# A two-layer graph network on one core: the 256-column products of the gather stages as two of 128 columns

## The chip, the cores and the metric

The kernel runs on one core of a Trainium2 chip, as one program. The metric is the device time in microseconds (us) of that core, taken from several executions. A profile of one execution shows what each engine did. The engines are called PE (TensorE, matmuls), PEld (its weight loads), DVE (VectorE), ACT (ScalarE), POOL (GpSimd) and SP (SyncE, which here only issues DMAs).

## The reference

3125 nodes with 128 features and 100000 edges (src, dst), sorted by dst. Two SAGE layers come first, then a layer norm, then two PNA layers, then a layer norm. What matters here is the sums over each node's incoming edges:

```python
# SAGE layer (twice)
summed = segment_sum(x[src], dst)
mean = summed / max(deg, 1)
x @ W_self + mean @ W_neigh + b
# PNA layer (twice)
h = (x @ W_pre[:F])[dst] + (x @ W_pre[F:])[src] + b_pre
mean = segment_sum(h, dst) / degc
mean_sq = segment_sum(h * h, dst) / degc
std = sqrt(relu(mean_sq - mean * mean) + EPS_VAR)
mx, mn = segment_max(h, dst), segment_min(h, dst)
agg = concat([mean, mx, mn, std])
out = concat([x, agg, agg * amp, agg * att]) @ W_post + b_post
```

## The kernel before

The nodes stand in NT = 25 blocks of NB = 125. A sum over edges is a product with a matrix of counts: for a block b of destinations and a block a of sources, the counts `A[:, slot, a, :]` (125 x 128, bf16) are the operand that is loaded into TensorE, and the rows of the source block stream past. A row in f32 is split into three bf16 parts c, so a block b takes 25 x 3 = 75 products that add up in one bank of PSUM (`acc[:, bank, 0:width]`). The helper is `add_block`; its line in the profile is L1190. It is called in three places:

- in the counting stage, with `width` = F = 128, inside a hardware loop;
- in `second_sums` (the second SAGE layer), with `width` = F, all 75 products of a block in a row;
- in `main_scan`, once for each PNA layer, with `width` = 2F = 256: columns 0 to 127 are the rows, 128 to 255 their squares. These two calls are the gather stages, the longest part of the program.

A gather stage is cut by hand into NSLOT = 91 slots. In a slot s TensorE does, in this order: `select` for slot s+1 (six products of 500 columns that pick rows for the maximum and minimum, L1305); at some slots the operands of a finished block (L1276 to L1279, f32, and transposes, L1266); some pieces of the sums ahead (a piece is one a, three products); `lift_absent` (two products of 500 columns, L1317); and more pieces behind it. The tables AHEAD and BEHIND fix the number of pieces: 0, 2 or 4 ahead, 5 to 7 behind. VectorE does `take_top` (L2228) after `select`, some rows of a running maximum (`scan_row`, L2275), `take_low` (L2246) after `lift_absent`, and more rows. `select` of slot s+2 waits for `take_low` of slot s, and `lift_absent` of slot s waits for `take_top` of slot s.

Beside this, POOL gathers the rows for `scan_row` from memory, four rows to a batch (`gather_rest`, L1129, an indirect DMA for each row), into a ring of six batches; ACT negates them (L947); SP writes the scanned rows out (L654), and the ring's place is free when that write is done. ACT copies the finished sums of a block (L786) and then loads the counts of the block after next (A<-counts). SP loads `picks` for `select`.

Of the kernel before, what the change touches and what calls it, by code (L numbers as in the profile page):

```python
# [14 lines left out]
F = 128  # L15
N = 3125
E = 100000
NB = 125
NT = N // NB
# [192 lines left out]
def gnn_kernel(nc, x, src, dst, w_self1, w_neigh1, b1, w_self2, w_neigh2, b2,  # L212
# [3 lines left out]
    with ctx:  # L216
        def sb(name, shape, dt=F32):
            return ctx.enter_context(nc.sbuf_tensor(name, shape, dt))
# [28 lines left out]
        XS = big[:].bitcast(BF16).rearrange("p (a c f) -> p a c f", c=3, f=2 * F)  # L247
        EXT = big[:, 0:NT * 2 * F].rearrange("p (a f) -> p a f", f=2 * F)
        A = sb("A", [P, 2, NT, P], BF16)
# [158 lines left out]
        acc = ps[:, 0:5]  # L408
# [765 lines left out]
        def _(pe):  # L1174
# [8 lines left out]
            def add_block(k, b, bank, slot, width, a0, a1):  # L1183

                if a0 == 0:

                    pe.wait_ge(sums_out, b + (NT * k + 1))
                for a in range(a0, a1):
                    for c in range(3):
                        m = nc.tensor.matmul(acc[:, bank, 0:width], A[0:NB, slot, a, :], XS[0:NB, a, c, 0:width],  # L1190
                                             start=a == 0 and c == 0, stop=a == NT - 1 and c == 2)
                if a1 == NT:
                    m.then_inc(summed, 1)

# [12 lines left out]
            def make_block(b, slot, first=False):  # L1207

                for j in range(PIECES):
                    pe.wait_ge(onehots, b * (2 * PIECES) + (2 * j + 3))  # L1210
                    pe.wait_ge(counted, b * PIECES + (j + 1))
                    h = (slot + j) % 2
                    for t in range(PT):
                        at = t // WT * CODES
                        m = nc.tensor.matmul(acc[:, h, at:at + CODES], hot_s[:, h, :, t],  # L1215
                                             hot_c[:, h, t],
                                             start=t % WT == 0, stop=t % WT == WT - 1)
                    m.then_inc(tallied, 1)
                    if first and 0 < j < COLS:
                        turn_windows(j)  # L1220
                    if not first and j > 1:
                        pe.wait_ge(counts_made, b * NG + (j - 1 - NG))
                        add_block(0, b - 1, 3 - slot, 1 - slot, F, (j - 2) * GT, (j - 1) * GT)
# [13 lines left out]
            with pe.Fori(0, NT // 2) as i:  # L1237
                make_block(i * 2 + 1, 1)
                make_block(i * 2 + 2, 0)
            pe.wait_ge(counts_made, NT * NG)  # L1240
            add_block(0, NT - 1, 2, 0, F, 0, NT)
            pe.wait_ge(pe_go, 4)
            nc.tensor.matmul(acc[:, 3, 0:P], tiny[:, 4:5].to_broadcast([P, P]), ident[:],
                             start=True, stop=True)
            pe.wait_ge(upper_made, 2)
            nc.tensor.matmul(acc[:, 3, P:2 * P], run_count.to_broadcast([P, P]), upper,
                             start=True, stop=True).then_inc(small_mm, 1)
# [74 lines left out]
            def main_scan(l):  # L1322
# [9 lines left out]
                def piece(b, a):  # L1332
                    if b == 0 and a % GT == 0:
                        pe.wait_ge(squares_ready, NG * l + a // GT + 1)
                    if a == 0:
                        pe.wait_ge(a_in[b % 2], 16 * (b // 2 + 1 + (k - 1) * ((NT + 1 - b % 2) // 2)))
                    add_block(k, b, b % 2, b % 2, 2 * F, a, a + 1)
# [1128 lines left out]
```

## Time and profile before

| | |
|---|---|
| median of 3 runs | 2146.79 us |
| lowest, highest run | 2123.44, 2160.79 us |
| profiled execution | 2106.36 us |
| its span, first to last instruction | 2104.6 us |
| PE busy | 1443.8 us (69%), 11250 matmuls |
| PEld busy | 1041.9 us (50%), 11250 loads |
| DVE busy | 1423.3 us (68%) |
| POOL busy | 804.5 us (38%) |
| mean granted clock of TensorE | 0.863 |

Busy shares are means over stages that differ much. A view by stage tells where an engine waits; the chain of waits tells what ended last. The two gather stages run from about 636 to 1262 us and from 1365 to 1985 us of the span. A matmul's recorded time holds the way of its last column through the array, so the cost of one in a row of many is the distance of the starts and not the mean.

### The profile page before, as it was taken

How to read it: one execution, taken by the hardware profiler on the slowest of the kernel's cores; microseconds unless marked ns; L12 is line 12 of the kernel's file. 1: busy time of each engine (PE TensorE's matmuls, PEld its weight loads, DVE VectorE, ACT ScalarE, POOL GpSimd, SP SyncE). 2: the span in 40 equal slices, each digit the busy share in tenths (PEclk: the TensorE clock that was granted, in tenths of full speed). 3: DMA queues.
4: the chain of work that ended last, by engine and by line, in shares of the span. 5: the costliest groups of instructions: out<-in, count | busy, mean ns of one | idle time of the engine just before them, and what ended most of it. 6: DMA issues, size and time to landing. Idle time of an engine off the chain costs nothing.

```text
span 2104.6 us, 30157 instructions
## 1 busy us (share of the span) xinstructions
PE 1443.8 (69%) x11250; PEld 1041.9 (50%) x11250; DVE 1423.3 (68%) x2879; ACT 502.3 (24%) x1074; POOL 804.5 (38%) x831
## 2 busy tenths in 40 slices
PE   0267777666974777877777865636777887787564
PEld 0156777655972444545554542424444554455432
DVE  7899999783425866666666754766655776676457
ACT  3357777500112111111111110310111111111101
POOL 4400000014006455556655624065545555565230
PEclk9879888886996988989988987978888998898876
DMA  5323333322443555555656532344555565565320
GB/s 119 94 110 140 140 140 140 125 87 93 161 139 98 178 171 192 178 186 184 200 167 197 184 113 63 92 141 161 176 181 176 187 201 182 170 219 170 139 63 25
DMA packets 126252, 309.57 MB, mean 147 GB/s; under 512 B 21744, under 2 KB 73408, under 8 KB 125742
## 3 DMA queue, kind: packets, MB, share of 16 engines
q1 hardware_dynamic: 75216, 145.00, 19.7%
q10 hardware_dynamic: 23470, 105.20, 14.2%
q0 software_dynamic: 27440, 57.77, 10.0%
q8 instruction: 69, 1.13, 0.2%
q14 instruction: 57, 0.47, 0.1%
HBM read 167.18 MB, written 140.75 MB: 146 GB/s over the span
## 4 chain that ended last, share of the span: by engine, by line
DVE 34%; PE 32%; issue 14%; another core or an unknown queue 12%; DMA 3%; ACT 2%; POOL 2%; ACTq 1%; DVEq 0%; POOLq 0%
PE ps L1190 16%; PE ps L1305 6%; DVE accs L2246 5%; DVE scanned L2275 4%; DVE accs L2228 4%; DVE scanned L1769 3%; DVE scanned L1766 3%; DVE scanned L1775 3%; PE ps L1317 2%; PE ps L1215 2%; PE ps L1405 1%; DVE S L1742 1%; DMA A<-counts 1%; ACT Y L756 1%
## 5 line engine op out<-in xcount | busy, mean ns | idle before, releaser
L1129 POOL DMA_INDIRECT scanned<-table,rest_idx x688 | 675.2, 981 | 712.1 <-DMA rest_history<-scanned 248.1
L1190 PE MATMUL ps<-big,A 125*128 125x128 bf16 (+1 forms) x7500 | 756.0, 257 | 60.9 <-issue 49.4
L1190 PEld LDWEIGHTS ps<-big,A 125*128 125x128 bf16 x7500 | 622.9, 103 | 190.9 <-issue 83.4
L1305 PE MATMUL ps<-S,big 126*128 126x500 bf16 (+1 forms) x1050 | 276.2, 406 | 251.7 <-DVE accs L2246 171.0
L2246 DVE TENSOR_TENSOR accs<-accs,ps 128x1000 f32<-128x1000 f32 (+1 forms) x154 | 166.7, 1083 | 342.7 <-remote 257.1
L2275 DVE SCALAR_TENSOR_TENSOR scanned<-scanned,rest_neg 128x256 f32<-128x256 f32 x688 | 331.7, 482 | 40.6 <-issue 7.6
L1305 PEld LDWEIGHTS ps<-S,big 126*128 126x128 bf16 x1050 | 101.1, 106 | 371.3 <-DVE accs L2246 187.5
L1215 PE MATMUL ps<-scanned 128*128 128x150 bf16 x1050 | 115.6, 252 | 76.3 <-DVE scanned L1775 75.4
L2228 DVE TENSOR_TENSOR accs<-accs,ps 128x1000 f32<-128x1000 f32 (+1 forms) x154 | 165.9, 1077 | 1.8 <-DVE sums_t L1883 1.3
L1148 POOL IOTA Y<- 128x784 int32 x1 | 0.8, 786 | 359.9 <-DVEq L2033 359.9
L1215 PEld LDWEIGHTS ps<-scanned 128*128 128x128 bf16 x1050 | 87.2, 132 | 92.7 <-issue 71.2
L811 ACT ACTIVATE A<-ps,tiny 128x450 bf16<-128x450 f32 x175 | 109.7, 635 | 87.6 <-PE ps L1215 47.8
L1317 PE MATMUL ps<-S,lift 128*128 128x500 bf16 (+1 forms) x350 | 102.5, 372 | 39.1 <-DVE accs L2228 19.6
L786 ACT COPY sums_t<-ps 128x128 f32<-128x128 f32 x50 | 13.3, 266 | 485.0 <-remote 271.6
L1405 PE MATMUL ps<-weights,scanned 128*128 128x384 f32 x200 | 90.8, 585 | 50.3 <-DVE scanned L2328 31.3
L947 ACT ACTIVATE scanned<-scanned 128x512 f32<-128x512 f32 x172 | 104.7, 620 | 57.6 <-DMA scanned<-table,rest_idx 49.1
L1769 DVE TENSOR_TENSOR scanned<-scanned,H 128x900 bf16<-128x900 bf16 x175 | 108.0, 617 | 0.0
L1766 DVE TENSOR_TENSOR scanned<-scanned,H 128x750 bf16<-128x750 f16 x175 | 94.5, 540 | 9.5 <-PE ps L1215 9.3
L796 ACT ACTIVATE A<-A,tiny 128x640 bf16<-128x640 bf16 x125 | 99.5, 818 | 0.4 <-DVE S L1742 0.4
L920 ACT ACTIVATE operands_t<-operands_t 128x128 f32<-128x128 f32 x50 | 15.5, 310 | 352.1 <-DVE operands_t L1876 247.3
L1775 DVE TENSOR_TENSOR scanned<-scanned,H 128x768 bf16<-128x768 bf16 x175 | 95.9, 548 | 0.0
L1405 PEld LDWEIGHTS ps<-weights,scanned 128*128 128x128 f32 x200 | 39.8, 221 | 76.9 <-DVE scanned L2328 38.8
(395 smaller groups left out, 1410.0 us busy)
## 6 DMA issues: line engine op xcount, KB each, us to landing
rest_history<-scanned SPq DMA_DIRECT2D x172, 512.0 KB
A<-counts ACTq DMA_DIRECT2D x75, 800.0 KB
S<-picks SPq DMA_DIRECT2D x60, 640.0 KB
picks<-S ACTq DMA_DIRECT2D x25, 800.0 KB
counts<-A ACTq DMA_DIRECT2D x25, 800.0 KB
scanned<-table,rest_idx POOLq DMA_INDIRECT x688
table<-Y SPq DMA_DIRECT2D x10, 320.0 KB, 2.6
S<-picks SPq DMA_DIRECT2D x10, 160.0 KB
```

What stands on the lines that cost most here:

```text
L1129: nc.gpsimd.indirect_dma_start(out=lanes[:, r, s, 0:F], out_offset=None, in_=tables[1 + l], in_offset=bass.IndirectOffsetOnAxis(ap=rest_id ...
L1190: m = nc.tensor.matmul(acc[:, bank, 0:width], A[0:NB, slot, a, :], XS[0:NB, a, c, 0:width], start=a == 0 and c == 0, stop=a == NT - 1 and ...
L1215: m = nc.tensor.matmul(acc[:, h, at:at + CODES], hot_s[:, h, :, t], hot_c[:, h, t], start=t % WT == 0, stop=t % WT == WT - 1)
L1305: m = nc.tensor.matmul(ps[:, bank + h, 0:len(blocks) * NB], XS[0:NB + 1, a, c, 0:F], pick[0:NB + 1, part % RING, 0:len(blocks), a % PART, ...
L1317: m = nc.tensor.matmul(ps[:, bank + h, 0:len(blocks) * NB], lift[:], pick[:, part % RING, 0:len(blocks), a % PART, 0:NB], start=False, sto ...
L1405: m = nc.tensor.matmul(acc[:, b % GT, 0:3 * F], lhs_ext[:, SLOT[b % GT], h * P:(h + 1) * P], weights[:, w + 4 + 3 * h:w + 7 + 3 * h, :] .r ...
L1766: v.tensor_tensor(plain_s[:, h, 0:NB], iota_s[:, 0:NB], by_step(lows, n).unsqueeze(1).to_broadcast([P, NB, PT]), ALU.is_equal)\
L1769: v.tensor_tensor(hot_c[:, h].rearrange("p t (c u) -> p t c u", u=2), iota_c.rearrange("p (c u) -> p c u", u=2).unsqueeze(1) .to_broadcast ...
L1775: v.tensor_tensor(hot_s[:, h], plain_s[:, h], by_step(heavy, n).unsqueeze(1).to_broadcast([P, P, PT]), ALU.mult)\
L2228: v.tensor_tensor(top[:, :, 0:cols], top[:, :, 0:cols], ps[:, bank:bank + 2, 0:cols], ALU.max)\
L2246: v.tensor_tensor(low[:, :, 0:cols], low[:, :, 0:cols], ps[:, bank:bank + 2, 0:cols], ALU.min)\
L2275: v.scalar_tensor_tensor(this, last, rest_neg[:, i:i + 1], this, ALU.add, ALU.max)\
```

## The change

Where `width` is 256, each product of `add_block` other than the first and the last of a block is issued as two of 128 columns, one over the rows and one over the squares, each with its own load of the same counts. The first product of a block (a = 0, c = 0) and the last (a = 24, c = 2) stay whole. Where `width` is 128, nothing changes.

```diff
                 for a in range(a0, a1):
                     for c in range(3):
-                        m = nc.tensor.matmul(acc[:, bank, 0:width], A[0:NB, slot, a, :], XS[0:NB, a, c, 0:width],
-                                             start=a == 0 and c == 0, stop=a == NT - 1 and c == 2)
+                        first, final = a == 0 and c == 0, a == NT - 1 and c == 2
+                        step = width if first or final else F
+                        for f in range(0, width, step):
+                            m = nc.tensor.matmul(acc[:, bank, f:f + step], A[0:NB, slot, a, :],
+                                                 XS[0:NB, a, c, f:f + step], start=first, stop=final)
                 if a1 == NT:
                     m.then_inc(summed, 1)
```

The order of TensorE's instructions in the middle of the first gather stage, three slots before the change. Rows of `big,A` are the products of the sums; a row with x15 stands for fifteen.

```order
L1305 MATMUL ps<-S,big 128x500 x6
L1190 MATMUL ps<-big,A 128x256 x6
L1266 MATMUL ps<-ident,operands_t 128x128 x2
L1317 MATMUL ps<-S,lift 128x500 x2
L1190 MATMUL ps<-big,A 128x256 x21
L1305 MATMUL ps<-S,big 128x500 x6
L1276 MATMUL ps<-weights,C 128x384
L1278 MATMUL ps<-weights,operands_t 128x384
L1279 MATMUL ps<-weights,operands_t 128x384
L1317 MATMUL ps<-S,lift 128x500 x2
L1190 MATMUL ps<-big,A 128x256 x15
```

Nothing has changed places afterwards; the same place, where a block ends and the next begins in the last rows (its line is L1193 now):

```order
L1308 MATMUL ps<-S,big 128x500 x6
L1193 MATMUL ps<-big,A 128x128 x12
L1269 MATMUL ps<-ident,operands_t 128x128 x2
L1320 MATMUL ps<-S,lift 128x500 x2
L1193 MATMUL ps<-big,A 128x128 x42
L1308 MATMUL ps<-S,big 128x500 x6
L1279 MATMUL ps<-weights,C 128x384
L1281 MATMUL ps<-weights,operands_t 128x384
L1282 MATMUL ps<-weights,operands_t 128x384
L1320 MATMUL ps<-S,lift 128x500 x2
L1193 MATMUL ps<-big,A 128x128 x28
L1193 MATMUL ps<-big,A 128x256
```

The 6, 21 and 15 products became 12, 42 and 28 and one whole, each on its old side of `lift_absent`; no wait and no other engine's instruction moved.

## Rows read from the trace of the kernel before

**Rows 1.** Gather stages by engine: busy us, instructions, clock, DMA share, GB/s

```profile
636.00:1262.00 626.00, 459.56 (x2824) 300.33 (x2824) 404.35 (x701) 98.05 (x250) 338.98 (x346) 0.88 0.52 172
1365.00:1985.00 620.00, 460.10 (x2818) 297.40 (x2815) 405.15 (x698) 96.74 (x248) 335.81 (x342) 0.87 0.53 175
```

**Rows 2.** Chain that ended last, by line, in the first gather stage

```profile
by line: another core or an unknown queue 17.8%; issue 14.9%; PE ps L1190 13.5%; PE ps L1305 9.8%; DVE accs L2246 9.1%; DVE scanned L2275 7.2%; DVE accs L2228 6.2%; PE ps L1317 3.7%; PE ps L1276 1.8%; PE ps L1278 1.7%; PE ps L1279 1.7%; DVE
```

**Rows 3.** PE groups by form: busy us, mean ns, idle before

```profile
L1190 PE MATMUL ps<-big,A 125*128 125x256 bf16 x3750 | 487.7, 282 | 22.9 <-issue 21.2 <-DVEq L2314 1.4
L1190 PE MATMUL ps<-big,A 125*128 125x128 bf16 x3750 | 268.3, 233 | 38.0 <-issue 28.2 <-ACT A L796 4.7 <-DMA A<-counts 4.0
```

**Rows 4.** Pieces of the chain at the full clock: start us, us

```profile
541.95 4.19 PE ps L1190 x75
...
811.84 1.64 PE ps L1190 x15
```

**Rows 5.** Timeline of PE, start us and us, a run of 128-column products at half clock

```profile
505.48 4.30 PE L1190 MATMUL ps<-big,A 125*128 125x128 bf16 x39 [0.44 <-issue]
509.61 0.60 PE L1482 MATMUL ps<-ident,sums_t 128*128 128x128 f32 x4
```

**Rows 6.** Pieces of the chain just behind a long wait

```profile
746.58 2.68 PE ps L1305 x6
749.26 2.56 PE ps L1190 x12
...
808.20 1.28 PE ps L1305 x6
```

**Rows 7.** Short stretches by engine, columns as in Rows 1

```profile
506.00:509.00 3.00, 3.00 (x31) 3.00 (x30) 0.00 (x0) 0.00 (x0) 0.00 (x0) 0.50 0.09 36
546.00:554.00 8.00, 8.00 (x141) 7.92 (x139) 5.80 (x18) 1.53 (x4) 0.00 (x0) 1.00 0.53 172
```

**Rows 8.** One line's loads: min/median/max ns

```profile
L1190 PEld LDWEIGHTS ps<-big,A x7500: 95/98/152, 120.6 to 1970.9; 125*128 125x128 bf16 x198
```

**Rows 9.** Waits in the first gather stage: us, times, longest

```profile
DVE accs L2246 <- remote: 121.3, 19, 13.3
```

**Rows 10.** The same view, PE alone: first gather stage, then the second

```profile
PE ps L1190 <- issue: 5.7, 11, 0.9
...
PE ps L1190 <- issue: 15.4, 29, 1.1
```

**Rows 11.** Timeline of POOL around one such wait

```profile
841.53 0.94 POOL L1129 DMA_INDIRECT scanned<-table,rest_idx  x1 [7.26 <-DMA rest_history<-scanned]
...
855.47 0.94 POOL L1129 DMA_INDIRECT scanned<-table,rest_idx  x1 [0.30 <-issue]
```

**Rows 12.** The same place on PE and DVE

```profile
850.07 1.80 PE L1190 MATMUL ps<-big,A 125*128 125x256 bf16 x15
...
855.09 1.20 DVE L2246 TENSOR_TENSOR accs<-accs,ps 128x1000 f32<-128x1000 f32 x1 [5.73 <-remote]
```

**Rows 13.** Stretches with POOL issuing without a pause, columns as in Rows 1

```profile
841.50:852.00 10.50, 9.22 (x61) 6.29 (x59) 7.46 (x14) 1.73 (x4) 8.03 (x9) 1.00 0.51 160
465.20:469.40 4.20, 3.88 (x66) 3.49 (x63) 4.03 (x6) 0.37 (x1) 3.29 (x4) 1.00 0.55 189
469.40:505.00 35.60, 18.21 (x132) 11.60 (x132) 21.40 (x27) 1.43 (x3) 26.61 (x25) 0.59 0.19 55
657.00:682.00 25.00, 10.34 (x39) 6.08 (x37) 11.62 (x16) 2.88 (x6) 16.49 (x16) 0.70 0.23 66
```

**Rows 14.** Chain in the second of these stretches, and at 672 us

```profile
482.43 0.58 PE ps L1190 x4
483.01 0.87 issue
...
672.03 8.86 another core or an unknown queue
```

**Rows 15.** DMA queues: packets, MB, share

```profile
q8 instruction: 69, 1.13, 0.2%
```

## Prediction

> **What bounds the kernel now.** I read the profile by stage first. The change touches only the two gather stages, 1246 us of the 2104.6 us span [rows 1]. There TensorE is busy 74% of the time and VectorE 65%; the DMA engines are at 0.52 and POOL at 54%. No engine is full, so busy shares alone don't say what a longer product costs. The chain of waits does: the products of the sums (L1190) are 13.5% of it in the first stage, the other matmuls of TensorE about 19%, the steps of VectorE on L2246, L2275 and L2228 about 22%, and 33% is "another core or an unknown queue" and "issue", in which no engine's recorded work ended last [rows 2]. The reader is to see two kinds of time here. One is steady slots of some 4.7 us, in which TensorE's instructions follow each other without a gap and VectorE fits in beside them. The other is long waits: VectorE's `take_low` waited 19 times, 121.3 us in all, for something that the trace doesn't name, in the first stage alone [rows 9].
>
> **Count.** Each stage has 25 blocks of 75 products, 3750 in both [rows 3]. Two of each block stay whole, so 3750 - 100 = 3650 products are cut and 3650 matmuls with 3650 loads are added. The columns that stream stay the same: 3650 x 256.
>
> **Cost of one cut, array time.** The trace has both forms, each with a load for every product. At the full clock fifteen 256-column products take 1.64 us, 109.3 ns each, and 75 products of 128 columns take 4.19 us, 55.9 ns each [rows 4], where the granted clock is 1.00, that is 2.4 GHz [rows 7]. Two halves are 111.7 ns, so a cut costs 2.4 ns. At half clock (0.50, 1.2 GHz [rows 7]) the 39 narrow products started 4.13 us before the next instruction, 105.9 ns each [rows 5], and twelve wide ones take 2.56 us, 213.3 ns each [rows 6]: two halves are 211.8 ns, no loss. With the mean clock at 0.88 and 0.87 [rows 1], about a quarter of the time is at half clock; I count the full price for all: 3650 x 2.4 ns = 8.8 us.
>
> **Cost of the second load.** The operand is the same one again, and no row shows a load that is left out, so it is really issued. A load is recorded with 98 ns in the median [rows 8], yet the 75 narrow products each had one and came every 55.9 ns [rows 4]. So two loads overlap, and the load's price is already in the 55.9 ns. This was measured in the second SAGE layer and not in a gather stage. The bound from above is that the loads stop overlapping when POOL gathers: 2 x 98 - 109.3 = 87 ns for each cut; from below a cut can't gain array time, since the columns are the same. I take the 2.4 ns, because the DMA load was alike (0.53 there, 0.52 and 0.53 in the gather stages [rows 1, 7]).
>
> The Trainium skill speaks against that: TensorE: Matmul & The Clock Gate, section Back-to-back issue gap, gives a sustained spacing of about 81 ns for a load with a 128-column product. By that figure a cut would cost 2 x 81 - 109 = 53 ns, an estimate of +193 us in all. The 55.9 ns of the trace decide against it here.
>
> **What lies on the path.** In steady slots TensorE's instructions have no gap between them, so all of its added time moves the next `select`. During the long waits of TensorE nothing is added, since the products are done by then. So I put 7 of the 8.8 us on the path (bounds 0 and 8.8).
>
> **Dispatch.** Inside runs of products TensorE waited for "issue" 11 times for 5.7 us and 29 times for 15.4 us, 21.1 us in both stages [rows 10]. If these pauses come by the instruction, twice as many instructions meet up to twice as many of them: 0 to +21 us. Half of such time is hidden beside VectorE, and I don't know whether the pauses come by instruction or by time, so I take +5. The instructions themselves are fetched by DMA; the larger of the two queues for them carried 1.13 MB at 0.2% of the engines' time [rows 15], and even doubled that is nothing beside 0.52. I cost it at nothing.
>
> **Other engines.** No wait is added. `summed` is still raised by the last product of a block, which stays whole; ACT's copy and the load of the next counts behind it move with TensorE. SP and POOL have the same instructions in the same order.
>
> **Sum.** +7 + 5 = +12 us. The profiled execution took 2106.4 us and would take 2118; the median of the runs is 2146.8, 40 above it, so the forecast there is 2159 us, 0.6% more. The runs differ by 37 us among themselves, so what I forecast can hardly be told from no change; about 2% is what a measurement of this kernel can tell.
>
> **Rivals.**
>
> *Long waits that come by the number of instructions (slower).* This is the one that I weigh most. Whenever POOL issues gathers without a pause, TensorE comes to a stand. From 841.53 to 855.47 us POOL issues one each 1.25 us [rows 11]; TensorE ran 61 products and 59 loads until 852 [rows 13], then `take_low` waited 5.73 us although `lift_absent` had been issued long before [rows 12]. In the second SAGE layer POOL began at about 465.2 us: TensorE ran 66 products and 63 loads in 4.2 us, then came in bursts of about four products with 0.87 us between them [rows 13, 14]. Some 120 to 130 instructions in both cases, but 10.5 us in one and 4.2 in the other: that looks like a budget of instructions. A slot has about 31 matmuls (2824 / 91) now and 51 after. The budget of about 120 (60 matmuls with their loads) would be used up after 1.2 slots and not 2.0. With 19 waits in 91 slots a cycle has 4.8 slots; 0.8 less makes 4.0, and the waits come 20% more often. I take 160 us of such waits in each stage (17.8% of 626 us is 111, and about half of "issue" [rows 2]): +64 us, with the array's 9 us 2220. It passes +43 us, the 2% bound, when the waits come 13% more often and nothing else is lost. Against it speaks the start of the first stage: from 657 to 682 us there are only 39 products and 37 loads in 25 us [rows 13], and still the chain has a wait of 8.86 us [rows 14]. There the stand can't come from many instructions; it goes by POOL's time. And in the bursts TensorE runs about a sixth of the time (4 x 55.9 ns of 1.45 us), as an engine would that is let in between POOL's instructions. Chance 0.19.
>
> *Loads exposed while POOL gathers (slower).* By the bound above 3650 x 87 ns = +318 us, 2465. It would have to show in the wide products too, and they keep 109.3 ns. Chance 0.02, and the Trainium skill's 81 ns would be a milder form of it (an estimate of 2340).
>
> *Clock (faster).* After each long wait TensorE runs at half clock: six products of `select` take 2.68 us and not 1.28, twelve of the sums 2.56 [rows 6] and not 1.31, together 2.65 us. With some 40 such waits in both stages that is 106 us. If more instructions in the same time kept the clock up in half of them, -53 + 12 gives 2106 us. The waits themselves would have to shorten for that, and nothing in the change does it. Chance 0.05.
>
> *Nothing to be seen.* All of the added time is hidden: 2147 us. Chance 0.24. The forecast itself has 0.50.
>
> **How the numbers follow.** 0.50 + 0.24 + 0.19 + 0.02 + 0.05 = 1. Forecast and "nothing" lie within 2%; a little of the forecast's upper side, where the pauses for "issue" double in full and lie on the path, goes over. Faster 0.05, same 0.73, slower 0.22. The low end is 2125, the unchanged time less the distance of the lowest run from the median, 23 us. The high end takes in the forecast's dearest terms (8.8 + 21 us, and the highest run 14 us over the median: 2191) and the first rival's 2220 with 15 us above it: 2235. That leaves out the faster rival, the exposed loads and the upper side of the first, some 0.15.
>
> **What the profile after would show.** Right: fifteen products become thirty in about 1.68 us at the full clock; the gather stages last 626 and 620 us plus 3 to 10 us each; the waits of `take_low` for the unnamed releaser stay near 19 in number and 121 us in the first stage. The first rival: their number goes up, the runs of POOL before each are shorter, and the chain has more than 17.8% of "another core or an unknown queue". Exposed loads: a pair of halves above 150 ns with the granted clock at 1.00. The clock rival: a mean clock above 0.88 in the gather stages. What would make the forecast wrong is above all the unnamed releaser, since I can cost the array but not what holds TensorE's results back.

## The result, and the profile after

The changed kernel took 2232.45 us (median of 4 runs, 2217.06 to 2252.84), the kernel before 2135.11 us beside it (4 runs, 2110.90 to 2160.79). The ratio is 1.052, 95% interval 1.037 to 1.067: slower, by some 97 to 110 us, where I had forecast +12. Ratios here and below are taken over the fast runs of each kernel, so they can differ a little from those of the medians. Later sessions matter for all that follows: in three of ten the kernel before took 2120 to 2134 us as here, in the other seven 1757 to 1760 us, with the same code; I call the first kind *sessions with the stand* and the second *sessions without it*, because what differs is whether TensorE comes to a stand while POOL gathers.

The page of the changed kernel, its own profiled execution (2252.8 us, 20 above its median; the profiled one of the kernel before, 2106.4 us, is an early one below its own, so the stages below differ by more than the medians do):

```profile
span 2251.1 us, 37457 instructions
...
PE 1545.9 (69%) x14900; PEld 1143.5 (51%) x14900; DVE 1425.8 (63%) x2879; ACT 502.0 (22%) x1074; POOL 800.9 (36%) x831
...
q8 instruction: 98, 1.61, 0.3%
...
PE 46%; DVE 24%; issue 18%; another core or an unknown queue 5%; DMA 2%; ACT 2%; POOL 2%; ACTq 1%; DVEq 0%; POOLq 0%
PE ps L1193 24%; PE ps L1308 8%; PE ps L1320 4%; DVE scanned L1772 3%; DVE scanned L1769 3%; DVE scanned L1778 3%; DVE accs L2249 3%; DVE accs L2231 2%; PE ps L1279 2%; DVE scanned L2278 2%; PE ps L1281 2%; PE ps L1282 1%; PE ps L1218 1%; PE ps L1408 1%
```

The same two lines of the kernel before:

```profile
DVE 34%; PE 32%; issue 14%; another core or an unknown queue 12%; DMA 3%; ACT 2%; POOL 2%; ACTq 1%; DVEq 0%; POOLq 0%
PE ps L1190 16%; PE ps L1305 6%; DVE accs L2246 5%; DVE scanned L2275 4%; DVE accs L2228 4%; DVE scanned L1769 3%; DVE scanned L1766 3%; DVE scanned L1775 3%; PE ps L1317 2%; PE ps L1215 2%; PE ps L1405 1%; DVE S L1742 1%; DMA A<-counts 1%; ACT Y L756 1%
```

The counts are right: 11250 + 3650 products and as many loads. The gather stages by engine, as in [rows 1]:

```profile
636.00:1321.00 685.00, 496.44 (x4637) 342.82 (x4635) 401.99 (x697) 94.57 (x244) 332.03 (x343) 0.84 0.48 157
1425.00:2128.00 703.00, 520.99 (x4644) 357.08 (x4642) 406.61 (x698) 97.07 (x248) 336.90 (x343) 0.82 0.47 155
```

The stages last 685 and 703 us where they lasted 626 and 620: +59 and +83, 142 of the 146 us between the two profiled executions. VectorE and POOL are busy as long as before. TensorE's idle time is up by 22 us in each, and its recorded busy time by 37 and 61 us, although the columns are the same: a product that comes singly counts with its whole record (0.22 us at 823.35 below) and not with the 0.056 us between two starts, and the granted clock is lower, 0.84 and 0.82 where it was 0.88 and 0.87. The view of the waits tells where its flow is broken. First stage, then the second, after the change:

```profile
PEld ps L1193 <- issue: 138.5, 176, 2.0
DVE accs L2249 <- remote: 137.1, 19, 15.2
...
PE ps L1193 <- issue: 106.9, 152, 2.4
...
PEld ps L1193 <- issue: 146.5, 201, 1.9
DVE accs L2249 <- remote: 139.5, 18, 10.8
PE ps L1193 <- issue: 110.7, 164, 1.8
```

The long waits of `take_low` (L2249 now) for an unnamed releaser did not become more frequent: 19 for 137.1 us, against 19 for 121.3 [rows 9]. The new waits lie *inside* the products of the sums. There TensorE waited for "issue" 316 times for 217.6 us, against 40 times for 21.1 us [rows 10]. They are not all added time, since other waits shrank: over the whole program `select` waited for `take_low` 171.0 us before and 31.7 us after.

```profile
PE ps L1305 <- DVE accs L2246: 171.0, 40, 12.2
```

```profile
PE ps L1308 <- DVE accs L2249: 31.7, 20, 14.9
```

One place shows the new kind of wait. POOL starts a run of twelve gathers at 813.4 us, and the windows and the timelines of TensorE and VectorE read:

```profile
813.40:817.90 4.50, 4.50 (x62) 3.65 (x60) 2.92 (x5) 0.00 (x0) 3.59 (x4) 1.00 0.84 272
817.90:828.30 10.40, 3.19 (x19) 1.55 (x17) 4.55 (x8) 0.83 (x2) 7.93 (x9) 0.89 0.61 197
```

```profile
816.19 1.84 PE L1193 MATMUL ps<-big,A 125*128 125x128 bf16 x30
820.32 1.45 PE L1308 MATMUL ps<-S,big 126*128 126x500 bf16 x6 [2.29 <-issue]
821.60 0.55 PE L1193 MATMUL ps<-big,A 125*128 125x128 bf16 x4
823.35 0.22 PE L1193 MATMUL ps<-big,A 125*128 125x128 bf16 x1 [1.19 <-issue]
824.06 0.22 PE L1193 MATMUL ps<-big,A 125*128 125x128 bf16 x1 [0.50 <-issue]
825.50 0.27 PE L1193 MATMUL ps<-big,A 125*128 125x128 bf16 x2 [1.22 <-issue]
```

```profile
819.07 1.20 DVE L2249 TENSOR_TENSOR accs<-accs,ps 128x1000 f32<-128x1000 f32 x1 [2.67 <-remote]
```

62 matmuls and 60 loads go through without a gap in 4.5 us, then 19 and 17 in 10.4 us. Two things hold TensorE up in turn. The gap before 820.32 ends when `take_low` does (819.07 + 1.20), and `take_low` itself had waited 2.67 us for a signal. From 821.60 on, with about 140 matmuls and loads done since 813.4, the products come one or two at a time with pauses of 0.5 to 1.2 us, and nothing that the trace names holds them. Before, 61 matmuls and 59 loads went through in 10.5 us of such a run [rows 13]: the same number, in more than twice the time.

### The profile page after: what moved, and what is told of

The parts are those of the page before. It is cut to its first block, busy times and chain, and to the rows that moved or that the text cites. A ratio compares the mean times of both kernels' runs of the same rounds, so it can differ in the third digit from the quotient of the medians.

```text
span 2251.1 us, 37457 instructions
## 1 busy us (share of the span) xinstructions
PE 1545.9 (69%) x14900; PEld 1143.5 (51%) x14900; DVE 1425.8 (63%) x2879; ACT 502.0 (22%) x1074; POOL 800.9 (36%) x831
## 4 chain that ended last, share of the span: by engine, by line
PE 46%; DVE 24%; issue 18%; another core or an unknown queue 5%; DMA 2%; ACT 2%; POOL 2%; ACTq 1%; DVEq 0%; POOLq 0%
PE ps L1193 24%; PE ps L1308 8%; PE ps L1320 4%; DVE scanned L1772 3%; DVE scanned L1769 3%; DVE scanned L1778 3%; DVE accs L2249 3%; DVE accs L2231 2%; PE ps L1279 2%; DVE scanned L2278 2%; PE ps L1281 2%; PE ps L1282 1%; PE ps L1218 1%; PE ps L1408 1%
## 5 line engine op out<-in xcount | busy, mean ns | idle before, releaser
L1193 PE MATMUL ps<-big,A 125*128 125x128 bf16 x11150 | 838.1, 232 | 255.5 <-issue 243.9
L1193 PEld LDWEIGHTS ps<-big,A 125*128 125x128 bf16 x11150 | 734.2, 104 | 381.6 <-issue 318.1
L2249 DVE TENSOR_TENSOR accs<-accs,ps 128x1000 f32<-128x1000 f32 (+1 forms) x154 | 166.9, 1084 | 463.1 <-remote 276.7
L1308 PE MATMUL ps<-S,big 126*128 126x500 bf16 (+1 forms) x1050 | 281.9, 408 | 92.3 <-issue 46.2
L1772 DVE TENSOR_TENSOR scanned<-scanned,H 128x900 bf16<-128x900 bf16 x175 | 109.3, 625 | 0.0
```

Of the source, the lines that this page charges most:

```text
L1193: m = nc.tensor.matmul(acc[:, bank, f:f + step], A[0:NB, slot, a, :], XS[0:NB, a, c, f:f + step], start=first, stop=final)
L1308: m = nc.tensor.matmul(ps[:, bank + h, 0:len(blocks) * NB], XS[0:NB + 1, a, c, 0:F], pick[0:NB + 1, part % RING, 0:len(blocks), a % PART, ...
L1772: v.tensor_tensor(hot_c[:, h].rearrange("p t (c u) -> p t c u", u=2), iota_c.rearrange("p (c u) -> p c u", u=2).unsqueeze(1) .to_broadcast ...
L2249: v.tensor_tensor(low[:, :, 0:cols], low[:, :, 0:cols], ps[:, bank:bank + 2, 0:cols], ALU.min)\
```

## The experiments

Three theories to begin with. **Theory 1**: a budget of TensorE's instructions while POOL issues gathers without a pause. **Theory 2**: the second load, or the array's work. **Theory 3**: the traffic of the transfers, which delays the fetch of the instructions.

### No-operations (e1, e8)

```diff
+                        if width == 2 * F and 0 < 3 * a + c < 3 * NT - 1:
+                            for _ in range(2):
+                                pe.nop(nofuse=True)
```

> The kernel before with two no-operations on TensorE behind each of the 3650 products that the change cuts: the same number of added instructions (7300) as the changed kernel has, and nothing more for the array to do. Theory 1 (while POOL issues gathers without a pause, TensorE has a budget of instructions, whatever they are): about as slow as the changed kernel, ratio to before 1.04 to 1.06, some +90 us. Theory 2 (the second weight load, or the work in the array, costs it): ratio 1.00 to 1.01. Between them, about 1.02 to 1.03, if a no-operation counts half, for instance because what counts is a matmul with its semaphore or its operands.

Measured: 1757.41 against 1758.42 us, ratio 0.999 (0.997 to 1.001). But the kernel before took 1758 us: there was no stand in that session. It was made again:

> The kernel before with 7300 no-operations on TensorE, once more: on three chips so far the kernel before took some 1758 us and the stand of TensorE was missing, so theory 1 had no case to be tried on. If on this chip the kernel before stands at some 2135 us: theory 1 (instructions of any kind) 1.04 to 1.06, theory 2 (loads or array work) 1.00 to 1.01. If it is at 1758 us again: 1.00.

The session had the stand: 2112.67 against 2120.36 us, ratio 1.007 (0.998 to 1.016). Yet neither run says anything of theory 1, because the no-operations never reached the chip. As built, TensorE's program of this kernel is byte for byte that of the kernel before, and the page of e8 shows it:

```profile
q8 instruction: 69, 1.13, 0.2%
```

That is the line of the kernel before [rows 15]. The 7300 instructions that the change adds took 29 packets more (98, on the page above), and the 3650 loads of e14, further down, 15 more (84). So e1 and e8 are the kernel before, measured once more, and whether instructions of any kind count or only matmuls and loads is open. The expectations of e10 and e15, further down, still take it as shown that no-operations cost nothing; it was not. What e8 does give is how far one program differs from itself with the stand: 0.7% between the groups of runs, and in one profiled execution, inside the products,

```profile
PE ps L1190 <- issue: 68.1, 94, 11.4
```

against 49.4 us in 66 waits in the other. The changed kernel has 243.9 us in 344 waits over the whole program, far outside that.

### Half of the cuts (e2)

```diff
-                        step = width if first or final else F
+                        step = width if first or final or a % 2 == 0 else F
```

> Only the products of the odd blocks of nodes (12 of 25 values of a, 36 of 75 products in a block of the sums, 1800 in both stages) are cut in two; the others stay whole. Theory 1 and theory 2 both give a cost that goes with the number of cuts: 1800/3650 of the 5.2%, ratio 1.026. A threshold (the longer block just misses a slot, so that one more stretch of POOL's gathers falls on it) would give either 1.00 or the full 1.05.

Without the stand: 1762.91 against 1758.42 us, 1.0027 (1.0006 to 1.0047). It says only that 1800 cuts cost some 4 to 5 us there.

### Plain transfers in place of the gathers (e3, e4, e9)

POOL's row gathers are taken out, and ScalarE issues, three batches ahead,

```diff
+                act.dma_start(lanes[:, r, :, 0:F],
+                              tables[1 + l][at:at + BATCH * P].rearrange("(s p) f -> p s f", p=P))\
+                    .then_inc(main.landed[r], 16)
```

> The kernel before, but POOL issues none of the row gathers: ScalarE issues one plain transfer of the same bytes (512-byte pieces, one batch of four rows per partition) three batches ahead. The rows are then not those that are asked for, so this leaves the gathering out and the output is not the reference's. Theory 1 (it is POOL's issuing without a pause that holds TensorE up): the waits for the unnamed releaser and most of the waits for issue go; they are some 33% of the chain in the first stage, so 100 to 300 us faster than before, ratio 0.86 to 0.95. Theory 3 (it is the traffic of the transfers that delays the fetching of instructions): the traffic is the same, ratio 0.98 to 1.00.

> The changed kernel with the same replacement of the gathers by plain transfers; the output is not the reference's for the same reason. Theory 1: the cuts cost only array time here, 3650 x 2.4 ns, so it is 0 to 15 us above the kernel before with plain transfers. Theory 2 (loads or array) and theory 3 (traffic delays the fetch of twice as many instructions): the 97 us between changed and unchanged kernel stay.

Both met a session without the stand: 1747.66 us (0.992, 0.990 to 0.995) and 1757.25 us (0.999, 0.997 to 1.001). They could not judge the theories on the stand, but their difference is the price of the change with POOL's row gathers taken away: +9.6 us, where I had worked out 8.8 for the array. By the two intervals that difference is uncertain by about 6 us.

> The cut in four (10950 products and loads added) with the row gathers replaced by plain transfers that ScalarE issues; the rows aren't those asked for, so the gathering is left out and the output is not the reference's. If the stand comes from POOL's issuing, it is missing here on any chip, and the ratio to the kernel with plain transfers (1748 us where the stand is missing) is 1.00 to 1.02. If loads of 64 columns are exposed (some 100 ns a load, 4 x 55 ns in place of 110 a product), up to +400 us on any chip. If POOL's gathers had merely hidden the cost in the run with the cut in four, this run shows it as the difference between 9 us (the cut in two) and more.

This one ran in a session with the stand, beside e8: 1821.45 us against 2120.36 for the kernel before, ratio 0.862 (0.856 to 0.868), *with* four products and four loads for each one. The waits:

```profile
DVE accs L2259 <- PE ps L1330: 82.2, 78, 3.4
...
PEld ps L1203 <- issue: 28.0, 32, 11.5
...
PE ps L1203 <- issue: 21.5, 22, 11.3
```

`take_low` (L2259) waits for the product of `lift_absent` now and for nothing unnamed, and the waits for issue in the products are 21.5 us for 18450 products, 11.3 of them a single wait. So the stand needs POOL's gathers; neither more loads nor more matmuls make one by themselves. That is against theories 2 and 3 (the bytes and the 512-byte pieces stayed).

Against the 1748 us of e3 the ratio is 1.04, and I had expected 1.00 to 1.02: a miss. A comparison with e18, the same cut with POOL's row gathers in a session without the stand, tells where the time is. The spans are 1812.3 and 1761.1 us. From the first to the last `select` the gather stages last 471 and 476 us here and 469 and 476 us there: in these stages the stand is gone altogether. The other 50 us lie outside them, ahead of the first stage, between the two and behind the second, where POOL's other gathers were left in. So e9 carries its own control: the session had the stand, and it is missing just where the row gathers were taken out.

### The changed kernel without the stand (e5)

> The changed kernel once more, unaltered. In the four runs before, the kernel before took 1758 us and not 2135, and neither the no-operations nor the plain transfers changed it by more than 1%, so the stand of TensorE was not there at all. If it is missing again, the changed kernel costs array time only: 3650 x 2.4 ns, ratio 1.00 to 1.01. If it is there (the kernel before at some 2135 us), the ratio is 1.04 to 1.07 again.

1762.18 against 1758.92 us, ratio 1.0023 (1.0002 to 1.0045): the change costs +3 us there. In its trace POOL gathers at the same pace, one each 1.25 us without a pause, and TensorE beside it:

```profile
820.08 0.94 POOL L1129 DMA_INDIRECT scanned<-table,rest_idx  x1 [0.30 <-issue]
821.33 0.94 POOL L1129 DMA_INDIRECT scanned<-table,rest_idx  x1 [0.30 <-issue]
```

```profile
820.42 1.84 PE L1193 MATMUL ps<-big,A 125*128 125x256 bf16 x29
822.10 1.44 PE L1308 MATMUL ps<-S,big 126*128 126x500 bf16 x6
823.37 1.51 PE L1193 MATMUL ps<-big,A 125*128 125x128 bf16 x24
824.71 0.38 PE L1320 MATMUL ps<-S,lift 128*128 128x500 bf16 x1
824.93 1.84 PE L1193 MATMUL ps<-big,A 125*128 125x128 bf16 x30
826.61 1.44 PE L1308 MATMUL ps<-S,big 126*128 126x500 bf16 x6
```

No gap: 30 products in 1.68 us, just what I had forecast for them, while POOL goes on. In such a session POOL's gathers hardly pause (the longest run has some 300, with no pause much over 1 us) and TensorE is not held. So POOL's gathers are needed for the stand but don't suffice.

What VectorE waits for can be followed one step further in the traces, since they hold the time of each signal (an update of a semaphore). Without the stand the signal of `lift_absent` comes 0.01 us after the recorded end of its last product, in all 182 slots of e5 and of e18, and so it does in e9. With the stand it comes over 1 us late in 79 of 182 slots of the kernel before (563 us in all, the longest 19.5), in 71 in e8 (481 us) and in 53 of the changed kernel (342 us). So the unnamed releaser of `take_low` is TensorE's own signal, delivered late; VectorE itself is not slow. And the change made these delays fewer, not more.

### The cut in four (e6, e10, e12, e15, e18)

```diff
-                        step = width if first or final else F
+                        step = width if first or final else min(width, F // 2) if width > F else F
```

> The cut doubled: each of the 3650 products of 256 columns is done as four of 64 columns with four loads, so 10950 products and loads are added and not 3650. If what is dear is the number of TensorE's instructions while POOL issues gathers (theory 1), and the kernel before stands at some 2135 us on this chip: three times the added instructions, ratio 1.12 to 1.16. Theory 2 (loads are exposed when the columns get few): a load is recorded with 98 ns and 64 columns stream in 27 ns at the full clock, so the four parts would take up to 4 x 55 ns and not 110, up to +400 us wherever it runs. Where the stand is missing (before at 1758 us) theory 1 gives 1.01 to 1.03, as much as the array time lies on the path.

> The cut in four once more, for a chip on which TensorE comes to a stand. No-operations did not cost anything there (ratio 1.007, interval 0.998 to 1.016), so if the stand goes by a count it is one of matmuls with their loads alone. If so, and if the kernel before stands at some 2120 us here: 10950 added pairs against the 3650 that cost 5.2%, ratio 1.12 to 1.16. If the cost goes by something else that the cut in two brings once (the place at which a slot ends against POOL's gathers), 1.03 to 1.07. If the stand is missing, 1.00 as in the first run of this kernel.

> The cut in four a third time, since both earlier runs of it met chips without the stand (ratio 1.00 both times). If the kernel before stands at some 2120 us here: a count of matmuls with loads gives 1.12 to 1.16 (three times the added pairs), a cost that comes once with any longer slot 1.03 to 1.07, a cost of the array's work alone 1.00 to 1.01. Without the stand 1.00.

> The cut in four in a session that, it is hoped, has the stand. The load-only run there cost 1.9% for 3650 loads, the cut in two 5.2% for 3650 loads and 3650 matmuls, no-operations nothing. A cost by the number of loads and matmuls, 0.013 to 0.014 us each of the added 21900, gives +290 us, ratio 1.12 to 1.16. If the cost saturates (TensorE is at the end of its budget in each run of POOL already), 1.05 to 1.10. Without the stand 1.00.

> The cut in four, for a session with the stand. The wide products showed that fewer loads and matmuls bring only 0.75% there: TensorE comes to its stand as late as before by the clock (about 12 us into a run of POOL), with fewer instructions done. With more of them (the cut in two) the stand comes earlier, after as many instructions as before (about 140). If that second limit is one of instructions, the cut in four reaches it after some 4 to 5 us of each run of POOL, and the ratio is 1.10 to 1.20. If the cost saturates, 1.05 to 1.08. Without the stand 1.00.

All five met sessions without the stand: ratios 1.0013, 1.0009, 1.0012, 1.0013 and 1.0018, each with an interval of +-0.002. Whether the cost with the stand goes on growing to +10% and more was not learned. What they do show is that 10950 more matmuls and loads cost some 2 to 3 us without the stand. The timeline of e18, at the full clock:

```profile
831.34 0.86 PE L1193 MATMUL ps<-big,A 125*128 125x64 bf16 x24
832.04 0.41 PE L1269 MATMUL ps<-ident,operands_t 128*128 128x128 f32 x2
```

24 products of 64 columns, each with its load, in 0.70 us: 29.2 ns each, so four parts take 117 ns and one of 256 columns 109 [rows 4]. Loads stay hidden down to 64 columns. The 7.5 ns more for each of 3650 products would be 27 us, of which 2 to 3 show: without the stand most of the array time is not on the path. The 81 ns for a load and a 128-column product, which the Trainium skill gives in TensorE: Matmul & The Clock Gate, section Back-to-back issue gap, is not what this kernel shows, with POOL gathering or without: it takes 56 ns (1.68 us for 30 in e5).

### Fewer products (e7, e11, e16, e17)

In the gather stages two neighbouring parts become one product of 512 columns. The second half of its result is not added to the first, so this kernel leaves the share of the middle part out of the sums.

```diff
-                        m = nc.tensor.matmul(acc[:, bank, 0:width], A[0:NB, slot, a, :], XS[0:NB, a, c, 0:width],
-                                             start=a == 0 and c == 0, stop=a == NT - 1 and c == 2)
+                        if width == 2 * F and c == 1:
+                            continue
+                        n = 2 if width == 2 * F and c == 0 else 1
+                        m = nc.tensor.matmul(
+                            acc[:, bank, 0:n * width], A[0:NB, slot, a, :],
+                            XS[0:NB, a, c:c + n, 0:width].rearrange("p c f -> p (c f)"), ...)
```

> The cut turned round: in the gather stages the first two of the three parts of a value (neighbours in memory) are one product of 512 columns into a whole bank, the third one of 256, so 50 products and loads a block and not 75, 1250 fewer in each stage with the same columns. The second half of the bank isn't added to the first: the share of the middle part is left out of the sums. Theory 1, with the stand of TensorE there: a third of the products gone, ratio 0.96 to 0.98. With no stand: ratio 0.99 to 1.00, since the columns are the same.

> The products of 512 and 256 columns once more (the middle part's share is left out of the sums), 2500 fewer matmuls with loads than before. With the stand there, a count of matmuls and loads gives about -0.7 x 5.2%, ratio 0.96 to 0.97; if the cost doesn't go by such a count, 0.99 to 1.01. If the stand is missing, 1.00 as in the first run of this kernel.

> The products of 512 and 256 columns (the middle part's share is left out of the sums), 2500 matmuls and 2500 loads fewer. A cost by the number of loads and matmuls gives -5000 x 0.0135 = -67 us, ratio 0.96 to 0.97, in a session that has the stand; if the budget isn't reached less often by it, 0.99 to 1.00. Without the stand 1.00.

Without the stand: 0.997 (0.994 to 0.999), 1.0005 and 1.0003: about nothing.

> The wide products once more, for a session with the stand (the middle part's share is left out of the sums). 2500 matmuls and 2500 loads fewer: by their number -67 us, ratio 0.96 to 0.97; by no count 0.99 to 1.01. Without the stand 1.00.

With the stand: 2127.14 against 2134.00 us, ratio 0.9925 (0.986 to 0.999), some 16 us less, and hardly more than the 0.7% by which one program differed from itself in e8. I had expected 67 less by the number of instructions: a miss. The trace tells why. POOL has a run of sixteen gathers from 1554.9 to 1575.0 us:

```profile
1565.37 0.59 PE L1322 MATMUL ps<-S,lift 128*128 128x500 bf16 x2
1565.79 1.79 PE L1193 MATMUL ps<-big,A 125*128 125x512 bf16 x10
1579.06 2.68 PE L1310 MATMUL ps<-S,big 126*128 126x500 bf16 x6 [11.47 <-DVE accs L2251]
```

```profile
1577.80 1.20 DVE L2251 TENSOR_TENSOR accs<-accs,ps 128x1000 f32<-128x1000 f32 x1 [12.07 <-remote]
```

```profile
1554.90:1567.30 12.40, 12.35 (x66) 6.85 (x65) 10.37 (x19) 1.83 (x4) 9.66 (x10) 1.00 0.79 260
1567.30:1575.00 7.70, 0.28 (x2) 0.00 (x0) 0.00 (x0) 0.00 (x0) 5.83 (x7) 0.73 0.20 51
```

TensorE had its instructions and ran all products it could without a gap; it was `take_low` that did not see `lift_absent`'s two products of 1565.37 until 1577.8, 2.8 us after POOL's run. The signal itself is recorded at 1577.78, 11.8 us after the end of the second product. That is the wait that the kernel before has at [rows 12]; there the signal is at 855.06, 4.8 us late. So two things are seen in the stand: TensorE's *signal* comes late (VectorE waits, for "remote"), and TensorE's *own flow* of matmuls and loads is held (it waits for "issue"). Fewer instructions can remove only the second, of which the kernel before had little, 21 us. Whether the two have one cause is not shown.

### A shorter lead of POOL, and loads alone (e13, e14)

```diff
-                    if n >= LANES_RING - 1:
-                        pool.wait_ge(main.scan_ops, BATCH * (n - LANES_RING + 1) + 1)
+                    if n > 1:
+                        pool.wait_ge(main.scan_ops, BATCH * (n - 2) + 1)
```

> The kernel before, but POOL may gather at most two batches of four ahead of VectorE's scan and not five, so it can't issue more than 8 gathers or so in a row; the gathers are the same. If the stand comes from POOL's issuing without a pause, and the kernel before stands at some 2120 us here: faster, ratio 0.85 to 0.95. If POOL's issuing does it whatever its pauses, 0.98 to 1.02. Where the stand is missing nothing is to be won, and where the rows now come late it is slower, 1.00 to 1.05.

With the stand: 2106.84 against 2122.77 us, 0.992 (0.987 to 0.998). A miss of size, and partly of design: I take it that after every stand VectorE catches up and opens POOL's gate several times at once, so runs of eight gathers and more remained (53 of them, 9.2 gathers on the mean and 16 at most, against 39 of 13.6 and 32 before). The waits show the shift:

```profile
POOL scanned L1129 <- DVE scanned L2275: 364.0, 99, 11.7
...
DVE accs L2246 <- PE ps L1317: 211.0, 73, 8.9
...
DVE accs L2246 <- remote: 87.9, 19, 8.2
```

87.9 us of unnamed waits and not 257.1 (over the program, 43 times before), but 211 for `lift_absent` in their place. It doesn't tell whether truly broken runs would end the stand.

```diff
+                        if width == 2 * F and 0 < 3 * a + c < 3 * NT - 1:
+                            nc.tensor.ldweights(A[0:NB, slot, a, :])
                         m = nc.tensor.matmul(...)
```

> The kernel before with one more load of the counts ahead of each of the 3650 products that the change cuts, and no more matmuls: the half of the change that is loads. With the stand there: 1.04 to 1.06 if loads make the cost, 1.02 to 1.03 if loads and matmuls count alike, 1.00 to 1.01 if only matmuls count. Without it 1.00 to 1.01; exposed loads would show on any chip as up to 3650 x 98 ns = 358 us.

With the stand: 2161.69 (four runs) against 2122.77 us, 1.0186 (1.0125 to 1.0247), +39 us for 3650 loads that do nothing. That is clear of no change, and about at the 2% that a measurement of this kernel can tell. It was not run without the stand, but its trace shows that the array takes no longer: fifteen products with two loads each start in 1.64 us at the full clock, as with one load each [rows 4].

```profile
825.00 1.80 PE L1192 MATMUL ps<-big,A 125*128 125x256 bf16 x15
826.64 1.44 PE L1307 MATMUL ps<-S,big 126*128 126x500 bf16 x6
```

So not the array's work is dear but the passing of the loads. The waits and one run of POOL from 1790.4 us:

```profile
PE ps L1192 <- issue: 151.1, 192, 11.3
```

```profile
1790.40:1796.80 6.40, 6.36 (x49) 4.99 (x82) 6.26 (x11) 0.83 (x2) 4.88 (x6) 1.00 0.64 241
1796.80:1805.30 8.50, 3.10 (x13) 1.27 (x24) 0.10 (x1) 0.00 (x0) 6.58 (x7) 0.80 0.51 167
```

131 matmuls and loads go through, fewer matmuls (49) than in the other examples and more loads (82), then the flow is held.

### The budget, counted over all runs of POOL

For each run of eight or more row gathers in the gather stages of these traces, with starts less than 2 us apart, I took the first gap in TensorE's starts from 2 us into the run to its end (over 0.7 us inside the products of the sums, over 2.5 us elsewhere), and the matmuls and loads from the start of the run to it. Medians, in sessions with the stand, with the middle half of the counts in brackets:

```
kernel            runs with a gap   of them inside   us to it   matmuls and loads to it
                                    the products
before            31 of 39           7               11.2       145 (128 to 170)
before, again e8  29 of 39           9               11.2       141 (125 to 155)
loads alone       38 of 43          29                9.2       149 (136 to 163)
changed           42 of 43          39                7.6       138 (121 to 156)
fewer products    29 of 37           0               12.9       132 (117 to 151)
short lead        36 of 53           5                7.7       117 (77 to 132)
```

In the first four rows, with POOL's usual lead, the time goes from 11.2 to 7.6 us, the median count stays at 138 to 149, and the first gap moves into the products. It is a tendency and not a sharp limit: the counts of single runs scatter widely, and with another bound for what ends a run of POOL (1.6 us) the medians fall to 131, 135, 137 and 125, in the same order of times. With fewer products the first gap is never one of the flow. The short lead doesn't fit as well; the rule for a gap also catches ordinary waits there, since VectorE waits for `lift_absent` much oftener.

## Why the prediction was wrong

- **The forecast fell at the step "Dispatch".** I took the 21.1 us of waits for issue inside the products, allowed them to double at most, and put +5 us on the sum. They became 217.6 us, ten times as much, and the kernel 97 to 110 us slower; the added waits are more than that because 139 us of `select`'s waits for `take_low` went at the same time. The reading that fits the counts above is that a cost that starts at a limit does not grow in proportion: the kernel before reached about 140 matmuls and loads at 11 us, just where the late signal or the end of POOL's run came anyway, so a second limit was hidden behind the first. The change put it at 7.6 us, ahead of it. The 21 us were the small visible part; [rows 13] had the 61 and 59 in plain sight.
- **The first rival had the right place, POOL's gathers and a number of TensorE's instructions, and its price (2220) is near the 2232 measured, but by luck and not by its working.** I had the long waits of `take_low` come 20% oftener. They stayed at 19 in the first stage and went from 24 to 18 in the second; 137.1 us against 121.3 in the first. The chain has *less* of "another core or an unknown queue" (5% against 12% of the whole), not more as I wrote; the added time is "issue", 18% against 14%, and the products drawn out between such pauses, L1193 at 24% against 16%. "Budget of about 120 instructions" was the useful part of it, at some 140 matmuls and loads; whether other instructions would count was not tested. What I held against it, the 39 products in 25 us at 657 us, is a place where the signal is late (by 4.6 and 7.7 us, for the products at 661 and 672 us), and that row does not speak against a budget.
- **Array time, 8.8 us: borne out in size.** +9.6 us between the kernels with plain transfers, +3 beside gathering POOL in a session without the stand. That 7 of it lie on the path with the stand was not tested, nor was the gain or loss at half clock.
- **Second load hidden in the array: right.** Even at 64 columns 29.2 ns a pair, and two loads beside one product of 256 columns keep the 109.3 ns (e14). The rival of exposed loads (2465) had its bound 87 ns a cut; the cut in four shows none. But "the load's price is already in the 55.9 ns" was wrong as a whole: with the stand a load costs 39 us / 3650 = 11 ns, whether the array hides it or not.
- **Fetch of the instructions at nothing: right.** q8 went from 69 to 98 packets [rows 15]; the cut in four has 155, costs 2 to 3 us without the stand, and in e9, in a session with it, its gather stages are as short as without it.
- **Clock: the rival (faster) fell.** The granted clock of the stages is 0.84 and 0.82, not above 0.88: longer stands, more time at the lower level.
- **"Nothing to be seen"** describes the sessions without the stand (1.0023), and the two levels of the same kernel are the reason why a profile of one execution could not have told me the price for all.

Of the 97 to 110 us, loads alone account for about 39 (e14), which leaves about 60 to 70 for the 3650 matmuls with the 9 us of array time; that part is a difference of runs of different sessions and was not run alone.

**What stays open.** What in the chip couples POOL's gathers to TensorE's flow and signals, and why only in some sessions; the cause of the slowdown is shown as far as POOL's gathers, the late signals and the broken flow, and not below that. One guess fits what was seen: that each matmul and load, and each signal, has to leave TensorE by a way that POOL's gathers hold, with room for some 140 entries. No run tried that way itself, and it may even belong to the recording of the trace, since every timed run is recorded. Whether instructions of other kinds count, whether many more instructions (the cut in four) cost more with the stand, and whether gathers truly broken up would remove it, was not learned. No version tried beats both kernels everywhere; the fewer products may gain 0.75% with the stand, but lack an addition that would have to be paid.

## What to carry to other kernels

A cost that sits at a limit is not seen in the trace of the kernel that stays just below it: when a trace shows an engine stop after about the same number of instructions in places of quite different length, ask how far the other parts of the kernel are from that number, and don't scale the small waits that are already there. Beside a queue that POOL feeds without pause, TensorE's instructions have a price of their own (11 ns a load here), though the array hides them; prefer fewer and wider products, and do not expect the reverse gain where another wait ends at the same place. And run the kernel before again beside each experiment: two levels of it, 2120 and 1758 us, would have made a 17% gain out of a program that is the same byte for byte. When an added instruction costs nothing, see first that it is there: the bytes of instructions that the program fetched (q8) stood still for the no-operations, and that line would have told it after e1.

## What the hardware showed that I had not expected

- The same program takes 1758 or 2120 to 2134 us from one session to the next, with intervals within a session of 0.2 to 0.9%. It does not go with the chip alone: on one chip the kernel before took 1760 us beside e6 and e7 and 2120 us beside e8 and e9. Until about 460 us of the span, where POOL's gathers for the next layers begin, the changed kernel's trace from a session with the stand and the one without it agree within 3 us.
- With the stand, TensorE's signal for products of 0.59 us was recorded 11.8 us after their end, and only 2.8 us after POOL's last gather (e17). Over both gather stages 79 of 182 such signals were over 1 us late in the kernel before, and none in e9, in a session with the stand but without POOL's row gathers.
- A load of 128 columns recorded with about 100 ns costs no visible array time beside a product of 64 columns that streams in 29.2 ns.
